# Recommender tower on one core: the fields written once at a step of ten columns, later transposes, and some squares on another engine

## What is computed

```python
e = jnp.stack([tbl_0[ids[:, 0]], ..., tbl_31[ids[:, 31]]], axis=1)      # (512, 32, 64)

def _cin_layer(X, prev_x, W, b):
    x_i = jnp.einsum('bmd,bhd->bmhd', X, prev_x).reshape(bsz, m * h, d)
    return jnp.einsum('oc,bcd->bod', W, x_i) + b[None, :, None]

prev_x = e
for W, b in ((W0, b0), (W1, b1)):                                        # W0: 128 x 1024, W1: 128 x 4096
    x_i = _cin_layer(e, prev_x, W, b)
    cin_outs.append(x_i.sum(axis=2))
    prev_x = x_i
z = jnp.concatenate(cin_outs, axis=1)                                    # (512, 256)
h = jnp.maximum(jnp.concatenate([z, dense_ctx], axis=1) @ W_top1 + b_top1, 0.0)
h = jnp.maximum(h @ W_top2 + b_top2, 0.0)
y = h @ W_top3
```

## Time and profile before

| | |
|---|---|
| time, median of 3 runs | 196.04 us (195.92 to 197.17) |
| span of the profiled execution | 194.2 us (the views give no time of its own beside it) |
| TensorE busy | 181.0 us, 93% |
| ScalarE busy | 144.9 us, 75% |
| VectorE busy | 137.3 us, 71% |
| GpSimd busy | 123.8 us, 64% |
| mean granted clock of TensorE | 0.991 |

### The profile page before, as it was taken

How to read it: one execution, slowest core, us unless ns; L and a number is a source line. 1 busy time by engine, 2 the same in 40 slices (tenths; PEclk the granted TensorE clock), 3 DMA queues, 4 the chain that set the end, 5 groups by cost and what they waited for, 6 DMA issues and landing times.

```text
span 194.2 us, 8803 instructions
## 1 busy us (share of the span) xinstructions
PE 181.0 (93%) x3815; PEld 157.7 (81%) x3815; DVE 137.3 (71%) x307; ACT 144.9 (75%) x349; POOL 123.8 (64%) x134
## 2 busy tenths in 40 slices
PE   6999999869669959999999999989999999999985
PEld 6999999749557738878898877868888879889984
DVE  2007799994499999999996499977765796693100
ACT  2499977549848997899868879979677797776333
POOL 3777787877777777777777777777777777000000
PEclk9999999999999997999999999999999999999999
DMA  6991111111123334427211411331141114010100
GB/s 182 311 339 33 27 29 24 29 25 30 27 51 64 84 83 75 118 54 177 50 30 30 81 30 30 50 58 30 32 83 32 30 32 75 17 23 14 29 3 0
DMA packets 16520, 12.26 MB, mean 63 GB/s; under 512 B 12513, under 2 KB 12897, under 8 KB 16482
## 3 DMA queue, kind: packets, MB, share of 16 engines
q1 hardware_dynamic: 12242, 7.44, 15.1%
q0 software_dynamic: 4096, 4.20, 11.2%
q10 hardware_dynamic: 144, 0.07, 0.1%
HBM read 9.59 MB, written 0.00 MB: 49 GB/s over the span
## 4 chain that ended last, share of the span: by engine, by line
POOL 47%; PE 31%; issue 16%; DMA 3%; ACT 2%; DVE 0%; ACTq 0%
POOL rows L626 47%; PE psum L458 13%; PE psum L220 7%; PE psum L545 3%; PE psum L527 3%; DMA rows<-table,idx 2%; PE psum L480 2%; PE psum L516 2%; PE psum L190 1%; DMA t_sb<-ids 1%; ACT t_sb L261 1%; PE psum L562 1%; DVE acc_sb L465 0%; ACT acc_sb L731 0%; ACT xx L271 0%
## 5 line engine op out<-in xcount | busy, mean ns | idle before, releaser
L626 POOL DMA_INDIRECT rows<-table,idx x128 | 123.1, 962 | 40.8 <-issue 38.7
L288 DVE TENSOR_TENSOR prod<-psum,xx 128x256 f32<-128x256 f32 (+3 forms) x160 | 85.7, 603 | 22.2 <-ACT xx L271 12.0
L261 ACT ACTIVATE t_sb<-psum 64x308 f32<-64x308 f32 (+1 forms) x180 | 76.4, 425 | 10.2 <-PE psum L205 3.9
L458 PE MATMUL psum<-coef,t_sb 128*64 128x128 f32 (+1 forms) x954 | 53.7, 275 | 0.0
L458 PEld LDWEIGHTS psum<-coef,t_sb 128*64 128x64 f32 (+1 forms) x954 | 47.4, 131 | 4.3 <-issue 4.1
L220 PE MATMUL psum<-prod,xx 64*32 64x154 f32 x1920 | 42.4, 300 | 2.0 <-ACT coef L731 0.9
L257 DVE COPY t_sb<-psum 64x308 f32<-64x308 f32 x64 | 30.8, 481 | 10.8 <-PE psum L220 9.5
L220 PEld LDWEIGHTS psum<-prod,xx 64*32 64x32 f32 x1920 | 30.7, 107 | 9.4 <-issue 5.9
L271 ACT ACTIVATE xx<-psum 128x256 f32<-128x256 f32 x32 | 12.3, 386 | 11.0 <-PE psum L190 10.6
L190 PE MATMUL psum<-ident,rows 128*128 128x128 f32 x64 | 13.6, 295 | 3.1 <-DVE prod L288 2.0
L358 DVE TENSOR_TENSOR t_sb<-t_sb,coef 128x64 f32<-128x64 f32 (+8 forms) x63 | 15.8, 321 | 0.2
(11 more groups left out here) (39 smaller groups left out, 120.9 us busy)
## 6 DMA issues: line engine op xcount, KB each, us to landing
rows<-table,idx POOLq DMA_INDIRECT x128, 2.7
t_sb<-t_sb SPq DMA_DIRECT2D x28, 64.0 KB
w_sb<-w1t SPq DMA_DIRECT2D x3, 512.0 KB, 6.9
t_sb<-w0x SPq DMA_DIRECT2D x1, 768.0 KB, 10.3
w0g_sb<-w0g SPq DMA_DIRECT2D x1, 512.0 KB, 9.2
w_sb<-top SPq DMA_DIRECT2D x2, 256.0 KB
w_sb<-top SPq DMA_DIRECT2D x1, 512.0 KB
w_sb<-w1t SPq DMA_DIRECT2D x1, 384.0 KB, 4.7
```

What stands on the lines that cost most here:

```text
L261: copy_t(act, lambda o, i: act.activation(o, i, ACT.Copy), 0, u, v)
L288: return dve.tensor_tensor(at(p, col, out), at(psum, XT[g] * BANK + a, first), at(x, x0 + b, second), ALU.mult)
L458: return pe.matmul(bank(ACC, half * O, O, j, width), t_sb[:, c:c + width], w, start=i < places, stop=i >= n - places, tile_position=(0, j))
L626: pool.indirect_dma_start(rows[:, c:c + D], None, table[:, :], bass.IndirectOffsetOnAxis(ap=idx[:, g:g + 1], axis=0))\
```

## The change

It has three parts.

First, `xx` goes away. The fields are copied once out of PSUM, straight into `prod` (`copy_fields`): a block is now 80 words (PITCH), and its eight fields stand at columns 1, 11, ..., 71, so that the 32 fields of a sample pair lie at one step of ten words over four blocks. The T matmuls read their weights there (`fields_of`), the products their second operand. The products fill the columns between: OUTER and INNER every second column in groups of four between two fields, the 32 far pairs every even column up to 62 (a half of them every fourth), SQUARE and NEXT together behind. The number of columns that the matmuls stream stays 77.

Second, in units 3 to 7 the squares (256 elements per half) are made by ScalarE out of the fields in `prod` (`act_squares`) and no longer by VectorE; the T matmuls of these units wait for them.

Third, from unit u = 9 on (LATE) the transposes of unit u + 1, and ScalarE's copy of its fields, stand behind the T matmuls, the contraction and `l1` of unit u.

```diff
+STEP = 10
+PITCH = STEP * GRAM
+AT_FAR, AT_FIELD, AT_OUTER, AT_INNER, AT_SQUARE, AT_NEXT, AT_ONE = 0, 1, 3, 43, 63, 72, 76
...
+        def fields_of(p, j, r):
+
+            return at(p, 4 * j * PITCH + AT_FIELD, [[STEP, M]], D * r, D)
...
-                                             xx[u % 2][D * r:D * (r + 1), x:x + M],
-                                             p[D * r:D * (r + 1), y + 2 * k * COLS:y + 2 * (k + 1) * COLS],
+                                             fields_of(p, j, r),
+                                             at(p, (4 * j + 2 * k) * PITCH, [[PITCH, 2], [1, COLS]], D * r, D),
...
-                pe.wait_ge(gram_ready, 2 * u + v // 2 + 1)
+                pe.wait_ge(fields_ready, 2 * u + v // 2 + 1)
                 pe.wait_ge(prod_ready, 2 * u + v // 2 + 1)
+                if u in ACT_SQUARES:
+                    pe.wait_ge(squares_ready, 2 * (u - ACT_SQUARES.start) + v // 2 + 1)
...
-            act.activation(xx[u % 2][:, x0:x0 + SUB // 2 * M], bank(XT[g], 0, SUB // 2 * M), ACT.Copy).then_inc(xx_ready, 1)
...
-            src = at(xx[u % 2], g * SUB // 2 * M, [[GRAM, 2 * SUB], [1, GRAM]])
-            dst = at(prod[2 * (u % 2) + g], PAIRS, [[COLS, 2 * SUB], [1, GRAM]])
-            act.activation(dst, src, ACT.Copy).then_inc(gram_ready, 1)
+            act.activation(at(prod[2 * (u % 2) + g], AT_FIELD, [[STEP, SUB // 2 * M]]), bank(XT[g], 0, SUB // 2 * M), ACT.Copy)\
+                .then_inc(fields_ready, 1)
+
+        ACT_SQUARES = range(3, 8)
+
+        def act_squares(act, u, g):
+
+            if u in ACT_SQUARES:
+                act.wait_ge(fields_ready, 2 * u + g + 1)
+                p = prod[2 * (u % 2) + g]
+                act.activation(at(p, AT_SQUARE, [[PITCH, 2 * SUB], [1, QUART]]), at(p, AT_FIELD, [[PITCH, 2 * SUB], [STEP, QUART]]),
+                               ACT.Square).then_inc(squares_ready, 1)
...
-                return dve.tensor_tensor(at(p, col, out), at(psum, XT[g] * BANK + a, first), at(x, x0 + b, second), ALU.mult)
+                return dve.tensor_tensor(at(p, col, out), at(psum, XT[g] * BANK + a, first),
+                                         at(p, AT_FIELD + b * STEP, [[STEP * d, n] for d, n in second]), ALU.mult)
...
-            pairs(NEAR, [[COLS, 2 * SUB], [1, 2 * FAR]], [[HALF, SUB], [1, QUART], [0, QUART]], 0,
+            pairs(AT_FAR, [[PITCH, 2 * SUB], [2, 2], [4, FAR]], [[HALF, SUB], [1, QUART], [0, QUART]], 0,
                   [[HALF, SUB], [0, QUART], [1, QUART]], QUART).then_inc(prod_ready, 1)
...
-                    if u < EVEN - 1:
+                    if u < LATE:
                         transpose_rows(pe, u + 1, g)
                     t_half(pe, u, g)
-                    if u == EVEN - 1:
-                        transpose_rows(pe, u + 1, g)
                     if b > 0:
                         contract(pe, b, 2 * (u % 2) + g)
                     if g == 0 and top_step(u, 7) is not None:
                         l1(pe, top_step(u, 7))
+                    if u >= LATE:
+                        transpose_rows(pe, u + 1, g)
```

More of the change, by code:

```diff
@@ L78, in build @@
         rows = sb("rows", UNITS * TILES * D)
-        prod = [sb(f"prod{n}", SUB // 2 * 4 * COLS) for n in range(4)]
-        xx = [sb(f"xx{n}", SUB * M) for n in range(2)]
+        prod = [sb(f"prod{n}", SUB // 2 * 4 * PITCH) for n in range(4)]
         w1_sb = sb("w1_sb", M * O)
@@ L131, in build @@
         xt_done = sem("xt_done")
-        xx_ready = sem("xx_ready")
-        gram_ready = sem("gram_ready")
+        fields_ready = sem("fields_ready")
         prod_ready = sem("prod_ready")
+        squares_ready = sem("squares_ready")
         fills_ready = sem("fills_ready")
@@ L185, in transpose_rows @@
             pe.wait_ge(gathered[u % UNITS][g], 16 * TILES // 2 * (u // UNITS + 1))
-            for ready in (xx_ready, prod_ready):
+            for ready in (fields_ready, prod_ready):
                 wait(pe, ready, 2 * (u - 1) + g + 1)
@@ L296, in products @@
-            pairs(NEXT, [[COLS, 2 * SUB], [1, 4]], [[QUART, 2 * SUB], [2, 4]], 0, [[QUART, 2 * SUB], [2, 4]], 1)
-            pairs(NEAR, [[COLS, 2 * SUB], [1, 2 * FAR]], [[HALF, SUB], [1, QUART], [0, QUART]], 0,
+            if u not in ACT_SQUARES:
+                pairs(AT_SQUARE, [[PITCH, 2 * SUB], [1, QUART]], [[1, 2 * SUB * QUART]], 0, [[1, 2 * SUB * QUART]], 0)
+            pairs(AT_NEXT, [[PITCH, 2 * SUB], [1, 4]], [[QUART, 2 * SUB], [2, 4]], 0, [[QUART, 2 * SUB], [2, 4]], 1)
+            pairs(AT_FAR, [[PITCH, 2 * SUB], [2, 2], [4, FAR]], [[HALF, SUB], [1, QUART], [0, QUART]], 0,
@@ L422, in build @@
         PARTS = (0, 13, 25, NEAR + 1, VCOLS)
-        T_COL = [*range(NEAR), COLS - 1, *range(NEAR, NEAR + FAR)]
+        T_COL = [AT_OUTER + STEP * a + 2 * b for a in range(4) for b in range(4)]
+        T_COL += [AT_INNER + STEP * m + 2 * n for m in range(2) for n in range(4)]
+        T_COL += [AT_SQUARE + n for n in range(QUART)] + [AT_NEXT + n for n in range(4)] + [AT_ONE]
+        T_COL += [AT_FAR + 4 * n for n in range(FAR)]
         def pack(sp, b):
@@ L762, in fields_in @@
             def fields_in(u, g):
[L763 to L766 removed]
+                copy_fields(act, u, g)
+                act_squares(act, u, g)
+            copy_fields(act, 2, 1)
             copies(1, 0)
[L768 removed]
             copies(1, 1)
@@ L833, in _ @@
             for n in range(8):
-                last = dve.memset(at(prod[n // 2], COLS * (1 + SUB * (n % 2)) - 1, [[COLS, SUB]]), 1.0)
+                last = dve.memset(at(prod[n // 2], PITCH * SUB * (n % 2) + AT_ONE, [[PITCH, SUB]]), 1.0)
             last.then_inc(fills_ready, 1)
```

64 lines of the change are left out of this document (22 added, 42 removed).

## The result

The changed kernel takes 223.65 us (median of 6 runs, 223.01 to 225.6); in the runs beside it the kernel before takes 196.6. The ratio is 1.138 with a 95% interval of 1.134 to 1.143: slower by 13 to 14%. The profiled execution took 223.31 us, with a span of 221.5. The forecast was 222.0, with a span of 220.0.

What follows compares the result with a forecast made beforehand. VectorE, almost without idle time, was taken to set the pace: dearer products end at 202.3 us, then 17.0 + 0.7 gives a 220.0 span, plus 1.84 around it, said as 222 us; own range 212 to 232, eight-in-ten range from 193.9 less 0.5.

Steps and rivals of the forecast that it cites:

- VectorE's second operand: VectorE's products: reads 40 bytes apart cost 1.82 ns an element, not 1.04; 1.70 us more per half over 2176 elements.
- The largest product: VectorE's 128x1024 product: near 2.0 us and not 1.21; its 16-byte writes counted only for the upper end of the excess.
- rival (c): VectorE's reads and writes both pay, 3.07 us per half; total 264 us; chance 0.09 (over 232 us).
- The price by the page: VectorE's strided reads at the Trainium skill's lower figure, 1.73 ns a column: about 215 us in all.
- The sum: Along VectorE: start at 67.1, ten halves of 4.82 us to 115.3, sixteen of 5.44 to 202.3, then 17.0 + 0.7: 220.0.
- The end: Behind VectorE's last products: 17.0 us to the span's end plus 0.7 for dear weight loads in the last half.
- Rival (b): Only TensorE's weight loads are dear, up to 0.75 us per half: 198 to 214 us; chance 0.12 with other partial prices.
- The sign that TensorE would wait for products in every half: Profile sign of a right forecast: TensorE waits for VectorE's products in every half; no size given.
- ScalarE's copy: ScalarE's field copy into every tenth column: 0.386 to 0.63 us; products up to 0.24 us later, counted as nothing.
- Part 2: Squares on ScalarE, units 3 to 7: VectorE loses 0.414 us and 256 strided reads in ten halves; TensorE's wait adds nothing.
- rival (a): The stride is free on all engines: 193.9 to 195.1 us, taken as 194.4; chance 0.32.
- Part 3: Late transposes from unit 9: up to 0.92 us off TensorE's wait; products 3 us later, covered; no gain where VectorE sets the end.

## Why the prediction was right

**VectorE's second operand.** Right, in kind and in size. The prediction took 1.82 ns an element from L347, a write of another engine; the 512-element product pays (1083 - 159)/512 = 1.80. That the price of another engine's writes would carry over to VectorE's reads was not argued beyond how far apart the words lie, and in so far the agreement is luck. Against the kernel before beside each, the ratio falls from 1.138 to 1.056 with the reads alone undone, to 1.125 with the far product's writes alone undone, and to 1.020 with both. So the reads by themselves hold more than half of the loss. Another 3 to 4% goes only when both are undone, since either of them holds the largest product, and 2% is left.

**The largest product.** The forecast of near 2.0 us held (2.06), and so did that of the 512-element one (1.09 against 1.083). But the step behind it named one cause where there are two. The prediction let the writes at 16 bytes enter only as an addition to the reads, for the upper end of the excess and for rival (c). Shown is that they cost as much by themselves as the reads do and vanish behind them. Rival (c) is out: the two don't add. So the duration was right, for a reason that was only half of it.

**The price by the page.** The Trainium skill, in "Vector Engine (DVE) Microarchitecture Reference", section 5.2, prices one hopping source at 1.73 and a hopping destination at 1.71 ns a column, a step of 24 words on both sources or the destination at 2.5, and says that read and write penalties only partly add. This case's lone instructions agree (1.72, 1.75, 2.45, and no addition at all in the pairs tried). The prediction's estimate from that page, 215 us, was low in part because products in the running loop pay more than lone ones, 1.80 and 1.86 ns on the largest two; the cause of that difference wasn't tried. The rest lies in the idle time and the end, below. The page's wording of full rate for adjacent pairs alone is contradicted by the step of two words (369 ns for 201 elements). The Trainium skill's "Advanced Engine Details and Errata", section Memory Cachelines, which asks for two hits on a line of 16 bytes, fits up to ten words: two words of a line of 16 bytes are touched at a step of two words, and one from four on.

**The sum.** Its terms, as forecast and measured: the fold's end 45.4 and 45.59; the T matmuls of unit 1 later by 2.7 and by 53.56 - 50.75 = 2.81; the start of the ten halves 67.1 and 67.03; ten halves of 4.82 and 4.81; their end 115.3 and 115.09. The sixteen later halves were to take 5.44 and end at 202.3; they end at 202.71, but by two errors that cancel. Without idle time a half is (202.71 - 115.09 - 1.71 - 0.55)/16 = 5.34, because INNER rose to 479 ns and not to 414 + 0.78 x 256 = 614. The squares did rise about so far: by the group's mean of 530 ns, (54 x 530 - 32 x 479)/22 = 604, an estimate. INNER reads two fields in turn and the same two again before it goes on, while OUTER goes through four fields and the far product through sixteen before one returns. Whether that is what spares INNER most of the price was not tried. The other way, the smallest product reads every second field, 80 bytes apart, and pays (407 - 159)/128 = 1.94. And VectorE idles 1.71 us before 160.49 and 0.55 before 193.03, which was counted at nothing. In the ten halves, too, two errors cancel: INNER takes 0.13 us less than forecast, and moving the squares takes 0.48 us off VectorE and not 0.62 (part 2). That the end of VectorE came within half a microsecond is luck, then, though the price is not far off in any term but INNER's.

**The end.** The prediction added 17.0 and 0.7 us, the latter for dear weight loads in the last half. That half takes 1.35 us against 1.29, so the 0.7 wasn't there. In its place VectorE's end and the last T matmuls lie 204.47 - 202.71 = 1.76 us apart, with a contraction that waits 1.43 us for the transfer that packs T. The span: 202.71 + 1.76 + 17.03 = 221.5.

**TensorE.** The load was to go to 2.04 us a half by L347's ratio of 1.82/0.86. It took 139/107 = 1.30 times as long and stayed almost behind the matmuls. Rival (b) falls with it: all weights near bring about 1 us by the medians. The sign that TensorE would wait for products in every half held in most halves, first at the transposes and from 131 us on at the T matmuls.

**ScalarE's copy.** The dear end, 0.63, was right (0.644). "I count nothing" fits a VectorE that is busy for 9.85 of 10 us; no run with the layout takes the copy's price away. Without VectorE's excess it can't be told from the rest of the 3 us that remain; which of it is the copy's stays open.

**Part 2.** Counted at -0.414 us and 256 strided reads in each of ten halves, 0.62 in all: 0.48 by the run without it, 5.0 us in time. The squares cost ScalarE 0.694 us each, the strided end of the estimate, and no wait for them is among TensorE's. The same part alone on the kernel before brings nothing: the wait for products that rival (a) would shorten by 1.2 us does shrink, from 1.95 to 0.52, but 1.30 us of waiting for ScalarE's copies of T take its place.

**Part 3.** "Covered by a unit of distance" was wrong: from 131 us on the T matmuls start right behind the products, so that distance is gone. It cost time at one place, unit 11, where the late order puts the first dense layer ahead of the transposes: 1.7 us of idle time on VectorE. On the kernel before the same order gains 0.6%, 1.1 us, near the 0.92 us that the prediction named for it, and the wait for gathered rows is gone from its trace.

**Rival (a)** is out with the durations. Even with VectorE's products back near their old durations this layout takes 200 to 201 us, not 194.4.

## What to carry to other kernels

Before a layout spreads words apart to save a copy, list every stream that will read or write them, each engine's, and price each one by its own step; a dear write can hide behind a dear read, and undoing one of them then brings little. Look first at the engine that has no idle time: here 0.2 us saved per half on ScalarE was paid with 1.6 us per half on VectorE. Moving work off an engine paid here only where that engine was full: the squares brought about 5 us in the changed kernel and nothing in the one before.

## What was not expected of the hardware

On VectorE and ScalarE a step of two words is free or nearly so, and from four words up to sixteen the price is about the same (505 ns for 203 elements read at four words on VectorE, 500 for 209 at sixteen), with three words between. At 24 words the reads cost still more (673 ns for 210 elements on VectorE, 724 on ScalarE). ScalarE's lone copies, with 150 to 157 elements written and 200 to 207 read at steps of 1, 2, 4 and 10 words, took 297, 304, 439 and 445 ns for the writes, 369, 382, 561 and 568 for the reads:

```profile
L836 ACT ACTIVATE prod<-coef 128x203 f32<-128x203 f32 x1 | 0.6, 561 | 0.0
...
L836 ACT ACTIVATE prod<-coef 128x201 f32<-128x201 f32 x1 | 0.4, 382 | 0.0
...
L836 ACT ACTIVATE prod<-coef 128x200 f32<-128x200 f32 x1 | 0.4, 369 | 0.0
```

On VectorE a spread read and a spread write cost as much as one of them (464 ns for 173 elements read at ten words and written at four, 464 for 174 at ten and ten). TensorE's weight load at 40 bytes took 139 ns for 32 columns against 107: 1.3 times, where the groups of VectorE's products took 1.28 to 1.70 times. And a step of ten words isn't dear for every product: INNER, which goes back and forth between two fields, took 479 ns against 414.
